# Output projection of the last four batches moved beside the choice of the tokens; their gate logits from the attention outputs and the product of the two weights

## The reference, cut to what matters

```python
def _L1_cond_ref(x, t, ...):
    ...
    o = jnp.einsum('bhnm,bhmd->bhnd', attn, v)
    o = o.transpose(0, 2, 1, 3).reshape(b, n, H * HD)      # H * HD = 1024
    x = x + o @ Wout.T                                     # 256 features
    tok = x.reshape(-1, d)
    gate = jax.nn.softmax(tok @ Wgate.T, axis=-1)          # 8 experts
    k_cap = bs // E                                        # 512
    vals, idx = jax.lax.top_k(gate.T, k_cap)
    ...
    g = _ln(tok[idx_flat], mlp_g, mlp_b).reshape(k_cap, E, d)
    y = ...                                                # two products per expert, with its own weights
    tok = tok.at[idx_flat].add(y.reshape(-1, d))
    return tok.reshape(x.shape)
```

## Time and profile before

| what | us |
|---|---|
| median of 3 runs (lowest, highest) | 1429.6 (1429.23, 1430.48) |
| profiled execution | 1431.61 |
| its span on the core | 1429.8 |
| PE busy in the span | 1370.5 |
| ACT busy | 1035.9 |
| DVE busy | 960.7 |
| POOL busy | 911.5 |

### The profile page before, as it was taken

The page is one execution under the profiler, slowest core; times in us unless marked ns, Lnnn a source line. Parts: engine busy times, 40 slices in busy tenths (PEclk is TensorE's granted clock), DMA queues, the critical chain, the costliest instruction groups (busy, mean ns, idle before and its releaser), DMA issues. The chain is left out here.

```text
span 1429.8 us, 30429 instructions
## 1 busy us (share of the span) xinstructions
PE 1370.5 (96%) x10795; PEld 1183.3 (83%) x10795; DVE 960.7 (67%) x2191; ACT 1035.9 (72%) x2703; POOL 911.5 (64%) x855
## 2 busy tenths in 40 slices
PE   7899999997899999999999999999999988999996
PEld 6799999996678887888888788788888777889896
DVE  5876667643776676677667667666755568678763
ACT  5556666565898889889888988988988732476662
POOL 2576666652678768867877876786787620354643
PEclk9899999999999999999999999999999999999999
DMA  5342222111100100110110011011011046145522
GB/s 159 114 129 67 68 67 68 49 45 30 38 9 30 53 23 31 53 45 9 52 46 31 30 53 36 18 53 45 9 45 46 30 148 253 45 104 156 137 35 30
DMA packets 61638, 89.04 MB, mean 62 GB/s; under 512 B 6144, under 2 KB 50992, under 8 KB 58800
## 3 DMA queue, kind: packets, MB, share of 16 engines
q1 hardware_dynamic: 53232, 75.82, 16.3%
q0 software_dynamic: 6144, 8.39, 3.6%
q10 hardware_dynamic: 2112, 2.88, 0.6%
HBM read 61.90 MB, written 25.18 MB: 61 GB/s over the span
## 5 line engine op out<-in xcount | busy, mean ns | idle before, releaser
L1386 POOL TENSOR_TENSOR prob<-prob,share_p 128x512 f32<-128x512 f32 x256 | 271.6, 1067 | 195.6 <-DVE share_p L1493 195.0
L1487 DVE TENSOR_REDUCE shift<-bank 128x2 f32<-128x512 f32 x256 | 164.7, 685 | 186.0 <-PE bank L1103 185.9
L1258 ACT ACTIVATE prob<-bank,shift 128x256 f32<-128x256 f32 x512 | 237.8, 479 | 64.3 <-DVE shift L1487 64.2
L147 PE MATMUL bank<-wqkv_h,rowsT_h 128*128 128x512 f32 x384 | 158.9, 414 | 2.8 <-PEq L311 1.7
L147 PE MATMUL bank<-wqkv_h,rowsT_l 128*128 128x512 f32 x384 | 151.5, 395 | 0.0
L147 PE MATMUL bank<-wqkv_l,rowsT_h 128*128 128x512 f32 x384 | 150.8, 393 | 0.0
L1115 PE MATMUL bank<-ident,prob 128*128 128x128 f32 x1024 | 142.7, 281 | 1.1 <-POOL prob L1386 1.1
L1374 POOL TENSOR_TENSOR landing<-landing,rq 128x512 f32<-128x512 f32 x128 | 131.1, 1046 | 8.4 <-DVE rq L1441 8.4
L1130 PE MATMUL bank<-pT,landing 128*64 128x256 f32 x1024 | 127.1, 388 | 1.7 <-ACT pT L1345 1.7
L1115 PEld LDWEIGHTS bank<-ident,prob 128*128 128x128 f32 x1024 | 109.5, 141 | 21.3 <-POOL prob L1386 3.7
L1258 ACT ACTIVATION_READ_ACCUMULATOR prob<-bank,shift 128x1 f32 x512 | 107.5, 210 | 0.0
(11 more groups left out here) (324 smaller groups left out, 4517.6 us busy)
## 6 DMA issues: line engine op xcount, KB each, us to landing
landing<-in_fc1s SPq DMA_DIRECT2D x6, 1024.0 KB
landing<-in_fc2s SPq DMA_DIRECT2D x6, 1024.0 KB
rows<-in_x SPq DMA_DIRECT2D x16, 256.0 KB, 2.9
xT<-in_xT SPq DMA_DIRECT2D x16, 256.0 KB, 2.7
x_again<-in_x SPq DMA_DIRECT2D x16, 256.0 KB, 2.8
x_rows<-x SPq DMA_DIRECT2D x16, 256.0 KB, 3.1
rows<-x_rows SPq DMA_DIRECT2D x16, 256.0 KB, 3.1
x<-x_rows SPq DMA_DIRECT2D x16, 256.0 KB, 2.9
```

The lines of the kernel that those rows point to most:

```text
L147: last = nc.tensor.matmul(out, a, b, start=(n == 0), stop=(n == 3 * len(ks) - 1))
L1258: last = nc.scalar.activation(prob[at][:, n, :], score_bank[side][:, n * T:(n + 1) * T], ACT.Exp, bias=shift[:, at, n:n + 1], scale=-1.0, ...
L1386: nc.gpsimd.tensor_tensor(prob[at][:, :, :], prob[at][:, :, :], share[:, at, :].unsqueeze(2).to_broadcast([P, TT, T]), ALU.mult).then_inc( ...
L1487: nc.vector.tensor_reduce(shift[:, s % 2 * 2 + side, :], score_bank[side][:, :].rearrange("p (n m) -> p n m", n=TT), AX, ALU.min).then_inc ...
```

## The change

The batches 12 to 15 are called late (`LATE = 4`).

*Attention.* Step 13 to 16 no longer hold the projection of the late batches, nor their x2, their statistics and norm and their stores. Their logits are made from x and the attention outputs o apart: x @ Wgate.T by the old fills, now on x as it is loaded, plus o @ (Wgate Wout).T. The product of the two weights, `wc`, is made once in pair 2 of step -1 (`logit_weights`, 16 products of float32 on PE, two instructions on DVE), from `woutT`, which SP loads in four transfers of 256 KB at the head of step -2. It is kept as a high and a low part side by side, 16 columns. `logits_of(b, half, its)` multiplies the o parts with it (two halves of eight products), ACT copies the 16x256 result to `from_o`, and the gate fill adds both parts with two more small products. The fills of x for batches 14 and 15 move to pairs 4 to 6 of step 15 (`CLOSING_FILLS`). SP writes the o parts of batches 12, 13 and 14 to DRAM (`keep_o`, eight transfers of 256 KB for each); those of batch 15 stay where they are.

*Routing.* PE makes x + o @ Wout.T of the late batches in row tiles: eight tiles of 24 products and one product with `ident` that adds x. Tiles 0 and 1 (batch 15) stand ahead of the transposes of the gates, the other six take the place of the idle products between the digits, four or three k-steps of three products each (`LATE_STEPS`). ACT takes each tile out of PSUM with its sum, makes the mean, the sum of squares and the norm; POOL makes the root. SP loads x and the o parts of batches 12 and 13 first, then the weight halves of expert 0 only, then the raw weights, then, when two more tiles are done, the o parts of batch 14 into the place of batch 12's (`load_late_o(3)`), and later the halves of expert 1. The first gather waits for the last of the late rows in DRAM.

To find room, `wout` parts, o parts, the first block's `w2`, `hid` and `h` parts and the experts' `hid` parts share one tile `kept`, and a few semaphores are used twice.

```diff
+LATE = 4
+LATE_FROM = NB - LATE
+LATE_ORDER = [NB - 1] + list(range(LATE_FROM, NB - 1))
+CLOSING_FILLS = {(NB - 1, 9): (NB - 2, "x2"), (NB - 1, 11): (NB - 2, "gates"), (NB - 1, 13): (NB - 1, "x2"), (NB, 3): (NB - 1, "gates")}
...
+                def keep_o(b, qs):
+                    for q in qs:
+                        wait(sp, o_lo, PAIRS, b, q + 2)
+                        for n, part in enumerate((o_h, o_l)):
+                            sp.dma_start(o_kept[b - LATE_FROM][n][:, q * T:(q + 2) * T],
+                                         o_part(part, q, b % 2, 2).bitcast(F32)).then_inc(o_stored, 16)
...
+                    if t == -2:
+                        for q in range(4):
+                            sp.dma_start(prob[q][:, :, :], a["woutT"][:, q * T:(q + 1) * T].rearrange("(k p) n -> p k n", p=P)).then_inc(wc_in, 16)
...
+                def logits_of(b, half, its):
+                    wait(pe, o_lo, PAIRS, b, 4 * half + 4)
...
+                    for k in range(4 * half, 4 * half + 4):
+                        for n, part in enumerate((o_h, o_l)):
+                            last = nc.tensor.matmul(chunk_bank[0][0:2 * E, 0:T], wc[:, k, :], part[:, o_at(k, its), :],
+                                                    start=(k == 0 and n == 0), stop=(k == PAIRS - 1 and n == 1))
...
                 def finish(t, its):
-                    fill(t, 1)
                     values(t - 1, PAIRS - 2, its)
                     transposes(t - 1, PAIRS - 1)
-                    project_last(PAIRS - 3, its)
+                    logits_of(t - 1, 0, its)
+                    values(t - 1, PAIRS - 1, its)
+                    logits_of(t - 1, 1, its)
                     fill(t, 3)
-                    values(t - 1, PAIRS - 1, its)
-                    project_last(PAIRS - 2, its)
-                    project_last(PAIRS - 1, its)
...
-                            if s in PROJ_PAIRS and live(t - 1):
+                            if s in PROJ_PAIRS and live(t - 1) and not is_late(t - 1):
                                 project(t - 1, PROJ_PAIRS.index(s), 1 - odd)
+                            if s == LATE_PAIR[False] and live(t - 1) and is_late(t - 1):
+                                logits_of(t - 1, 0, 1 - odd)
+                                logits_of(t - 1, 1, 1 - odd)
...
+LATE_STEPS = [4, 3, 3, 3, 3] * 3
+TAKEN_IN, SPREAD_IN, NORMED_IN = {3: 2, 5: 3, 8: 4, 10: 5, 13: 6}, {4: 2, 6: 3, 9: 4, 11: 5, 14: 6}, {1: 0, 2: 1, 6: 2, 8: 3, 11: 4, 13: 5}
...
+                    for i, b in enumerate(LATE_ORDER):
+                        sp.dma_start(late_x[i][:, :, :], x1_rows[bass.ds(b * T, T), :].rearrange("(t p) d -> p t d", p=P)).then_inc(late_in[i], 16)
+                        if i in (1, 2):
+                            load_late_o(i)
+                    load_halves(sp, w1_in, (w1_h, w1_l), halves[0:2], 0)
+                    load_halves(sp, w2_in, (w2_h, w2_l), halves[2:4], 0)
+
                     load_raw(sp, w1_raw, a["fc1s"], EARLY, 0, 0)
                     load_raw(sp, w2_raw, a["fc2s"], EARLY, 0, 1)
                     sp.dma_start(b1[:, :], a["b1s"]).then_inc(b1_in, 16)
                     sp.dma_start(b2[:, :, :], a["b2s"].unsqueeze(0).to_broadcast([P, E, D])).then_inc(b2_in, 16)
+                    for i, b in enumerate(LATE_ORDER):
+                        if i > 0:
+                            sp.wait_ge(late_made, NB + TT * (i + 1))
+                        if i == 1:
+                            load_late_o(3)
+                        if i == 2:
+                            load_halves(sp, w2_in, (w2_h, w2_l), halves[2:4], 1)
+                        if i == 3:
+                            load_halves(sp, w1_in, (w1_h, w1_l), halves[0:2], 1)
+                        sp.wait_ge(late_normed, NB + TT * (i + 1))
+                        for rows, tile, last in ((x2_rows, late_n[i], last_rows), (out, late_x[i], last_out)):
+                            sp.dma_start(rows[bass.ds(b * T, T), :].rearrange("(t p) d -> p t d", p=P),
+                                         tile[:, :, :]).then_inc(last if i == LATE - 1 else late_stored, 16)
...
                 def _(pe):
-                    idle_products(6)
+                    def late_step(i, k):
+                        j, rows = i // TT, slice(i % TT * P, (i % TT + 1) * P)
+                        high, low = late_o[j]
+                        if k == 0 and i % TT == 0:
+                            pe.wait_ge(late_in[j], 16 + (16 if j == 0 else 48))
+                        if k == 0 and i >= 2:
+                            pe.wait_ge(late_taken, NB + i - 1)
+                        for m, (o, w) in enumerate(((high, wo_h), (high, wo_l), (low, wo_h))):
+                            nc.tensor.matmul(late_bank(i), o[:, k, rows], w[:, k, :], start=(k == 0 and m == 0), stop=False)
+                        if k == HW // P - 1:
+                            nc.tensor.matmul(late_bank(i), ident[:, :], late_x[j][:, i % TT, :], start=False, stop=True).then_inc(late_made, 1)
+
+                    for i in range(TT):
+                        for k in range(HW // P):
+                            late_step(i, k)
+                    done = TT * (HW // P)
                     pe.wait_ge(gated, 1)
                     for i in range(2):
                         last = nc.tensor.transpose(banks[0][:, i * P:(i + 1) * P], flat(gates)[:, i * P:(i + 1) * P], ident[:, :])
                     last.then_inc(tr_gates, 1)
-                    idle_products(6)
...
-                        idle_products(6)
+                        for _ in range(LATE_STEPS[n]):
+                            late_step(done // (HW // P), done % (HW // P))
+                            done += 1
...
+                        if first(later):
+                            pool.wait_ge(last_rows, 16 * (LATE_FROM + 1))
```

More of the change, by code:

```diff
@@ L1065, in step @@
                         load_piece(0, 0)
+                    if is_late(t - 1) and live(t):
+                        keep_o(t - 1, (0, 2, 4, 6))
                     b = t - 2
-                    if live(b):
+                    if live(b) and not is_late(b):
                         wait(sp, out_normed, TT, b, TT)
```

299 lines of the change are left out of this document (196 added, 103 removed).

## The result

The changed kernel takes 1461.0 us (median; 1460.1 to 1461.4) against 1429.4 us of the kernel before in the same job, a ratio of 1.022 [1.020, 1.023]. Slower was forecast, by 13.5 us; it is 31.6 us. The profiled execution took 1460.1 us with a span of 1457.7 us. The two traces differ by 27.9 us of span.

The account below looks back on a forecast made before the run. PE was taken to bound attention until ACT becomes late, and one chain of DVE, ACT and PE the routing block. Start +4.0, rest of attention -12.2, routing +21.7 gave +13.5: 1443 us, range 1430 to 1450.

Parts of the forecast that it names:

- The start: Start of attention: woutT loads ahead of batch 1's rows +2.6 us, weight product net +1.4, together +4.0.
- Steps 13 and 14: Attention: pairs 2 and 3 shorten to 6.15 and 3.8 us; 4.8 us saved for both, extra gate products +0.5.
- Step 15: Attention's step without next-batch chunks: pairs 2 to 7 shorten as projection products go, 4.0 us saved.
- the end: End of attention: o part 1.06 us earlier, fewer products behind it, finished at 1163.1 instead of 1167.08; 3.9 us saved.
- Routing: Routing block 21.7 us longer (10 to 25): count 11 20.6 later, other digits 0.3, tail 0.8.
- the landing: Routing, digit 10: batch 14's o parts land at +44.8 us of the block (42.5 to 47), PE standing 9 us.
- rival 1: Routing: batch 14's o parts overtake b2 and the stores, landing at +40.7, 4 us less: 1439; chance 0.06.
- Rival 2: Routing: no stall at digit 10, SP reaching the load much sooner; routing costs 11.7, time 1433; chance 0.12.
- Rival 3: Faster: PE time is the currency all through attention, 19.1 us off instead of 12.2: 1426; chance 0.15.
- Rival 4: Routing: late work does not fit between digits, counts delayed 0.5 us or batch 13's parts late: 1451 or more; chance 0.07.
- The signs: Announced: first Sign 14 to 16 us into routing, digit-10 wait 7 to 11, block 57 to 64, starting 6 to 11 earlier.
- The range: Whole kernel: 8 in 10 range of 1430 to 1450 us, leaving out rival 3 and a part of rival 4.

Follow-up runs that it names:

- experiment 6: Kernel with the rows of batch 1 first, weight product also cut into eight parts ahead of step -1's waiting transposes: 1451.5 us, before 1430.4.
- experiment 5: Changed kernel with the four woutT loads issued behind the rows of batch 1 instead of ahead: 1453.1 us, before 1430.6.
- experiment 7: Changed kernel with the 16 logit products and the weight product in pair 3 of steps 13 and 14 instead of pair 2: 1457.0 us, before 1430.6.
- experiment 8: Changed kernel with ten idle 128x128 products at the end of pair 3 of steps 0, 13 and 14: 1456.2 us, before 1431.4.
- experiment 1: Changed kernel with batch 14's o parts loaded earlier, ahead of both raw weights: 1453.5 us, before 1430.6, ratio 1.015.
- experiment 3: Changed kernel with tiles 0 and 1 no longer ahead of the gates' transposes, all eight tiles between the digits: 1458.0 us, before 1430.6.
- the last three kernels: All cures plus later loads of b2, expert 1's halves and raw weights: 1428.5 us; also four tile-0 k-steps ahead: 1426.5; also idle products in step 0: 1429.1.
- experiment 4: Changed kernel with only the routing block rebuilt: all eight tiles between the digits, SP's list reordered: 1445.7 us, before 1430.4.
- experiment 9: Changed kernel with rows first, weight product in parts, logit products in pair 3 and rebuilt routing together: 1433.2 us, before 1430.4, ratio 1.0016; later variants reordered loads further.

## Why the prediction was wrong in its size

Five terms were too small, in the two traces: the start by 4.4 us, steps 13 and 14 by 3.9, routing by 3.2, the end of attention by 1.3, and steps 0 to 12, which had no term, by 1.9. Step 15 and the expert block come to -0.3. Together 14.4 us, from +13.5 to +27.9.

**The start (+4.0, bounds 0 to 8; +8.4 measured, +9.7 with step 0).** The loads were sized at +2.6 and measured +3.3. The weight product was netted to +1.4, on the ground that it stands before transposes that already wait; measured about 3 (experiment 6 against 5). In one piece it held back the first transposes, for which ACT waits, so PE's waits for ACT behind it stayed (4.5 us in four places); that this is why is read from the trace, and only the 3 us are tested. And the clock was left out: a longer stand of PE was counted as a delay and not as a fall to 1.2 GHz, 2.1 us in the chunks. The prediction priced that very effect at the head of the routing block (1.5 us) and not here.

**Steps 13 and 14 (-4.3; -0.4 measured).** This step failed in kind. It asked after each engine's busy time in a pair, PE's 2.4 and ACT's 3.8 us, and took the larger. What binds is a latency over two pairs: scores, minimum, exponential, share, POOL's product, transposes, 6.2 us from a pair's start. Emptying pair 3 only moved the wait into pair 4: the two take 12.33 us whether pair 3 holds nothing more, the 16 logit products (experiment 7) or ten idle ones (experiment 8). At full clock it leaves 1.3 us a step (0.99 in pair 2, 0.33 in pairs 3 and 4); the fall of the clock in step 14 took 1.65 back, and pair 1 of step 14, where the fills of x2 and gates stand now, grew by 0.7 (5.50 to 6.18). Step 0 of the trace of before held the two lengths at full clock, 3.81 and 8.51 us; the fall of the clock it did not show.

**Step 15 (-4.0; -3.8) and the end (-3.9; -2.6).** Right in step 15. At the end 2.4 us pass between ACT's two copies (1167.65 to 1170.06), where 1.3 was put. Half of the difference is the clock, 0.68 on average in 1168 to 1170: the gate products of the second row tile take 1.51 us and those of the first 0.96.

**Routing (+21.7; +24.9).** The mechanism was right at each point that it named: head, first Sign, place, transfer and tail of the stall. Only the landing was mis-sized, +48.4 instead of +44.8. SP's wait for the first raw weight ended 1.6 us later, and from there the parts took 15.7 us and not 13.8. That second part arose before `b2` had landed, 9.6 us after the wait and not 7.4. While it and the first stores were under way, from 1208 to 1211, the queue moved 246 to 282 GB/s, against 418 to 449 from 1212 to 1217; whether the stores were the cause is not tested. The Trainium skill (DMA: Bandwidth & Descriptors, section Queues, rings and completion order) allows a later transfer to finish before an earlier one; here the store issued 0.5 us after the low o part landed together with it (12.2 and 12.7 us from their issues), and `b2`, issued before, ahead of both (8.7 us). No transfer is seen to pass another by more than the 0.1 us to which these times are given, and rival 1 did not occur. Rival 2 (no stall) was wrong: the stall goes only when the load is moved (experiment 1), and even then the time is 1453.5 us and not 1433. Rival 3 (PE's time is the currency) fell with the 6.2 us. Rival 4 had a time that fits, 1451 or more, and a cause that does not: the counts stayed 1.9 us apart, as before, and batch 13's parts were not late.

**The signs.** The first Sign at +14.8 was inside what was announced. The wait of 12.7 us lay above its 7 to 11, the block of 64.1 just above its 57 to 64, and the block's start, announced 6 to 11 us earlier than before, came 3.5 us later: this sign alone says that attention, and not routing, was the larger miss.

**The range.** All three stages came out at the bad end of their bounds or beyond: start 8.4 us where 8 was the end, attention 6.8 us saved where 8 was, routing 24.9 where 25 was. The bad ends add up to +25, 1455 us, and the range, 1430 to 1450, was made as if they would not meet. They met in part by one cause: 2.1 us in the chunks, 1.3 in step 0, 1.65 in step 14 and 0.55 at the gates are the clock that PE is granted after it has stood, and it had no term in attention.

What is not shown: how much of a median the fall of the clock makes. It is seen in single profiles (steps 0 and 14 in the changed kernel and with the halves last, steps 13 and 14 with the o parts early, none with the rows first), and each trace is one execution. The mean clock of every execution points the same way: with the halves last the fastest has 0.982 and 1446.2 us, the slowest 0.976 and 1453.9, and in experiments 1, 3 and 5 too the slowest has a lower clock than the fastest.

## What to carry to other kernels

Before you take work off the engine that is never idle, look in the same trace for a stretch that already lacks that work; here step 0 held the pair lengths that pairs 3 and 4 of steps 13 and 14 would get at full clock. Cost a removed product by the latency of the chain across iterations and by the clock that the thinner engine is granted, not by its busy time. And where work is moved into a stretch, write the issuing engine's list out as a queue with the landing of each transfer, and count the issues themselves where a block ends with them: the same work, with that list reordered and the added products moved to where PE waits, took 1426.5 to 1429.1 us in the last three kernels instead of 1461.

## What the runs showed of the hardware that was not expected

PE's granted clock fell from 1.00 to 0.50 behind two short stands, 1.38 and 0.87 us, with scores and transposes between them, and was back at 1.00 about 3 us later. The fall comes and goes with identical code before it: pair 4 of step 0 takes 9.84 us in the changed kernel and 8.50 in experiment 1, and over all profiles it is 10 of 26 such places. The Trainium skill (TensorE: Matmul & The Clock Gate, section Part 1: The HAM clock gate) says that the number of products at the slow clock varies between runs of one kernel. It says so of a kernel's start; these traces show the like in the middle of one. With ten idle products of 128x128 in the first stand the clock stayed at 1.00 in all three places, and they cost nothing (12.33 us for both pairs, with them and without).

A block can end with the issues of SP alone: in experiments 4 and 9 five transfers of 1 MB, issued in 3.7 and 3.4 us behind the last store, held the next block back until 0.46 us after the last issue, though nothing waited there for their landing.
